# A 64-batch cross attention and mixture kernel: the cross attention's phase turned by half a step

## The reference, cut to what matters

```python
q = (layernorm(x) @ Wq).reshape(B, Nq, 8, 64)
k = (context @ Wk)...; v = (context @ Wv)...
attn = softmax(einsum('bihd,bjhd->bhij', q, k) * 64 ** -0.5)
x = x + einsum('bhij,bjhd->bihd', attn, v).reshape(B, Nq, 512) @ Wo + bo

h = layernorm(x)
rw = gating(h, sim_matrix, gates)          # 16 experts, softmax over the active ones, the best 2 if none is
q, k, v = [einsum('bte,bted->btd', rw, einsum('btc,ecd->bted', h, w)) for w in (q_proj, k_proj, v_proj)]
attn = causal_softmax(q @ k.T / 8) @ v
x = x + einsum('bted,edc->btc', attn[:, :, None, :] * rw[..., None], o_proj)
```

## Time and profile before

| | |
|---|---|
| median of 3 runs | 3160.13 us (3153.86 to 3162.54) |
| the profiled execution | 3160.58 us, its span 3158.8 us |
| TensorE, VectorE, ScalarE, GpSimd busy | 2698.7, 2240.8, 1329.0, 1095.7 us |
| the mean granted TensorE clock | 0.929 of full speed |
| DMA | 440.76 MB, 140 GB/s |

### The profile page before, as it was taken

The page is one execution under the profiler, slowest core; times in us unless marked ns, Lnnn a source line. Parts: engine busy times, 40 slices in busy tenths (PEclk is TensorE's granted clock), DMA queues, the critical chain, the costliest instruction groups (busy, mean ns, idle before and its releaser), DMA issues. The chain is left out here.

```text
span 3158.8 us, 54354 instructions
## 1 busy us (share of the span) xinstructions
PE 2698.7 (85%) x17290; PEld 2574.5 (82%) x17290; DVE 2240.8 (71%) x6487; ACT 1329.0 (42%) x4594; POOL 1095.7 (35%) x1675
## 2 busy tenths in 40 slices
PE   4688889888888889888888889898888888898897
PEld 3688878888888878888888888788888888788886
DVE  5476777676777777777676767676777767676774
ACT  4443444343443444444343444443444434444431
POOL 0142333342333333343333333333433423333443
PEclk6799999999999999999899999898999999999998
DMA  6554444444444454445453444534454544444431
GB/s 155 166 161 127 147 146 133 150 144 143 135 153 129 150 147 129 150 150 153 125 153 119 150 136 137 152 123 144 148 154 126 162 126 147 144 129 147 150 104 38
DMA packets 296557, 440.76 MB, mean 140 GB/s; under 512 B 36752, under 2 KB 208720, under 8 KB 288080
## 3 DMA queue, kind: packets, MB, share of 16 engines
q1 hardware_dynamic: 296272, 437.28, 45.8%
HBM read 257.91 MB, written 179.31 MB: 138 GB/s over the span
## 5 line engine op out<-in xcount | busy, mean ns | idle before, releaser
L1263 DVE SCALAR_TENSOR_TENSOR acc<-bank_b,rw,acc 128x192 f32<-128x192 f32 x1792 | 647.0, 407 | 273.1 <-PE bank_b L506 269.1
L504 PE MATMUL bank_b<-wqkv_hi,x2T_lo 128*128 128x384 f32 (+1 forms) x2048 | 742.6, 363 | 93.2 <-DVE acc L1263 92.2
L506 PE MATMUL bank_b<-wqkv_hi,x2T_hi 128*128 128x384 f32 (+1 forms) x2048 | 718.0, 351 | 0.0
L505 PE MATMUL bank_b<-wqkv_lo,x2T_hi 128*128 128x384 f32 (+1 forms) x2048 | 717.7, 350 | 0.0
L1539 POOL TENSOR_TENSOR mixs_lo<-mix,mixs_hi 128x512 fp32r<-128x512 f32 x256 | 362.1, 1434 | 437.1 <-ACT mixs_hi L996 437.1
L504 PEld LDWEIGHTS bank_b<-wqkv_hi,x2T_lo 128*128 128x128 f32 x2048 | 409.7, 200 | 119.5 <-DVE acc L1263 105.5
L1458 POOL TENSOR_TENSOR pow_out<-pow_in,expo 128x2 f32<-128x2 f32 (+1 forms) x128 | 111.1, 868 | 907.9 <-DVE pow_in L1104 621.0
L505 PEld LDWEIGHTS bank_b<-wqkv_lo,x2T_hi 128*128 128x128 f32 x2048 | 408.4, 199 | 0.0
L506 PEld LDWEIGHTS bank_b<-wqkv_hi,x2T_hi 128*128 128x128 f32 x2048 | 405.6, 198 | 0.0
L940 ACT ACTIVATE probs<-bank_a,s_max 128x77 f32<-128x77 f32 x1024 | 318.2, 333 | 71.0 <-DVE s_max L1191 70.9
L1304 DVE TENSOR_TENSOR mix<-rw_all,late_tiles 128x512 f32<-128x512 f32 x256 | 267.3, 1064 | 80.3 <-DMA rw_all<-rw_dram 78.1
(11 more groups left out here) (201 smaller groups left out, 6371.5 us busy)
## 6 DMA issues: line engine op xcount, KB each, us to landing
gq<-g_dram SPq DMA_DIRECT2D x64, 1232.0 KB, 8.5
g_dram<-draft SPq DMA_DIRECT2D x168, 462.0 KB
uo<-u_dram SPq DMA_DIRECT2D x64, 1024.0 KB
rw_all<-rw_dram SPq DMA_DIRECT2D x128, 512.0 KB, 6.1
u_dram<-draft SPq DMA_DIRECT2D x172, 308.0 KB
xt<-in_x_dram SPq DMA_DIRECT2D x64, 256.0 KB, 5.9
out_dram<-mix SPq DMA_DIRECT2D x64, 256.0 KB, 2.3
uo<-u_dram SPq DMA_DIRECT2D x64, 208.0 KB
```

The source lines that it names most:

```text
L504: nc.tensor.matmul(dst, lhs[1], rhs[0], start=start, stop=False)
L505: nc.tensor.matmul(dst, lhs[0], rhs[1], start=False, stop=False)
L506: return nc.tensor.matmul(dst, lhs[0], rhs[0], start=False, stop=stop)
L1263: V.scalar_tensor_tensor(acc[:, t, k, :], src, rw[:, t, e:e + 1], acc[:, t, k, :], ALU.mult, ALU.add).then_inc(b_evac, 1)
```

## The change: what it does

It moves the cross attention by half a step against the mixture. In step i TensorE now works on XT of batch i+2 (`nxt`), and on S, PT and Y of batch i+1 (`ahead`). The score tiles stand in the first half of the step, one each behind fills 7, 8, 9 and 10, among the quarters of `c_y`; PT0 to PT2 among fills 12 to 14; Y between fill 2 and `c_pv`, where the scores were. LayerNorm 2 of batch i moves to the step's start. The jobs are dealt anew over the places, M3 being filled in one step of three (before: in all three), M2 in all (before: in two).

Other parts: ScalarE now issues the transfers of the routing weights itself, the write right behind the transposition, which moves to the step's first half, and the spread load behind PT1's copy (`c_rw`). LayerNorm 2's result, qkv and p2 now lie in `mix`, the small attention's operands in `mixs`, and `x2` in three tiles in turn, so GpSimd's copy of it (line 1474) goes. `b_route` is cut in two, the causal scores' maximum between them. Group 0 becomes a full group of three batches, and the last group holds batch 63 alone but is computed as three. The diff, cut:

```diff
-    GROUPS = (B - 1) // GB + 1
+    GROUPS = (B + GB - 1) // GB
...
-    A_ORDER = ("E0", "PT0", "PT1", "PT2", "E1", "Y", "E2", "E3", "M1", "XT", "M2", "M3", "S0", "S1", "S2", "S3", "L1", "L2")
+    A_ORDER = ("E0", "S0", "S1", "S2", "S3", "E1", "E2", "PT0", "PT1", "PT2", "E3", "M1", "XT", "M2", "M3", "Y", "L1", "L2")
...
+    JOBS = ({"E0": ("g", 3), "E1": ("k", 3), "E2": ("g", 4), "E3": ("g", 5), "M1": ("v", 0), "M2": ("g", 6), "L1": ("g", 7),
+             "L2": ("v", 1)},
...
+        gm = i // 3 + (2 if kind == "ct" or i % 3 == 2 and kind != "u" else 1)
...
+        qkv = mix[:, 0:2, :].rearrange("p a b -> p (a b)")[:, 0:NT * QKV].rearrange("p (t f) -> p t f", t=NT)
+        x2n = mix[:, 2:2 + NT, :]
+        p2 = mix[:, 4:6, :].rearrange("p a b -> p (a b)")[:, 0:3 * P]
+        k_hi, q_stack, k_stack = [mixs[0][:, k, :] for k in range(3)]
+        v2 = [mixs[0][:, 4 + k, :].rearrange("p (t a d) -> p t a d", t=NT, a=2) for k in range(2)]
+        p2T = [mixs[1][:, 2 * k:2 * k + 2, :].rearrange("p a b -> p (a b)")[:, 0:3 * P].rearrange("p (a b) -> p a b", a=3)
+               for k in range(2)]
...
+            def step(i):
+                def turn(slot):
+                    if job(i, slot):
+                        gm, kind, f = job(i, slot)
+                        if kind == "g":
+                            store_g(gm, f)
+                        elif kind == "u":
+                            store_u(gm, f)
+                if i % 3 == 2 and i // 3 + 3 < GROUPS:
+                    load_ctx(i // 3 + 3)
+                turn("E0")
+                if on(i + 2) and i + 2 > 0:
+                    load_x(i + 2)
+                if on(i + 2):
+                    load_g(i + 2)
+                turn("E1")
+                if i % 3 == 2 and on(i + 1):
+                    load_u(i + 1)
+                if on(i - 2):
+                    store(i - 2)
+                turn("E2")
+                turn("E3")
+                turn("M1")
+                turn("M2")
+                turn("M3")
+                if i % 3 != 1 and on(i + 2):
+                    load_u(i + 2)
+                turn("L1")
+                turn("L2")
...
                 do(before, b_qkv, 6)
-                turn("E0", (j_v, 2), (j_ct,), (j_k, 3))
+                turn("E0")
+                do(before, c_rT)
                 do(before, b_qkv, 7)
                 do(earlier, c_y, 0)
+                fill("S0", ahead, a_s, 0)
                 do(before, b_qkv, 8)
+                fill("S1", ahead, a_s, 1)
                 do(earlier, c_y, 1)
-                fill("PT0", now, a_pT, 0)
-                fill("PT1", now, a_pT, 1)
+                do(before, b_qkv, 9)
+                fill("S2", ahead, a_s, 2)
+                do(before, b_qkv, 10)
+                fill("S3", ahead, a_s, 3)
                 do(earlier, c_y, 2)
-                fill("PT2", now, a_pT, 2)
+                do(before, b_qkv, 11)
+                turn("E1")
                 do(earlier, c_y, 3)
-                do(before, b_qkv, 9)
-                turn("E1", (j_u, 2), (j_k, 0), (j_g, 4))
-                do(before, b_qkv, 10)
-                fill("Y", now, a_y, 0)
-                do(before, b_qkv, 11)
-                turn("E2", (j_u, 3), (j_k, 1), (j_g, 5))
-                do(now, a_y, 1)
+                turn("E2")
                 do(before, b_qkv, 12)
-                turn("E3", (j_v, 3), (j_g, 0), (j_v, 0))
+                fill("PT0", ahead, a_pT, 0)
+                fill("PT1", ahead, a_pT, 1)
                 do(before, b_qkv, 13)
+                fill("PT2", ahead, a_pT, 2)
                 do(before, b_qkv, 14)
+                turn("E3")
                 do(before, b_qkv, 15)
-                turn("M1", (j_u, 4), (j_g, 1), (j_g, 6))
-                fill("XT", ahead, a_xT)
-                do(before, c_rT)
                 do(now, b_xT, 0)
                 do(now, b_xT, 1)
-                turn("M2", (j_u, 5), (None,), (j_g, 7))
+                turn("M1")
+                fill("XT", nxt, a_xT)
+                turn("M2")
                 do(before, c_qk)
                 do(now, b_qkv, 0)
-                turn("M3", (j_u, 6), (j_k, 2), (j_v, 1))
+                turn("M3")
                 do(now, b_qkv, 1)
                 do(before, c_s)
                 do(now, b_qkv, 2)
-                fill("S0", ahead, a_s, 0)
-                fill("S1", ahead, a_s, 1)
-                fill("S2", ahead, a_s, 2)
+                fill("Y", ahead, a_y, 0)
                 do(before, c_pT)
-                fill("S3", ahead, a_s, 3)
+                do(ahead, a_y, 1)
                 do(before, c_pv)
                 do(now, b_qkv, 3)
                 do(now, b_qkv, 4)
-                turn("L1", (j_u, 7), (j_g, 2), (j_u, 0))
+                turn("L1")
                 do(now, b_qkv, 5)
-                turn("L2", (None,), (j_g, 3), (j_u, 1))
-
-            for r in (1, 2):
-                step(-1, r)
-            for i in range(B + 2):
-                step(i // 3, i % 3)
+                turn("L2")
...
             def c_rT(n):
-                act.wait_ge(c_fill, c_at(n, C_RT))
-                if not (known(n) and n == 0):
-                    act.wait_ge(rwT_out, 16 * n)
-                nc.scalar.activation(rwT[:, :], bank_c(C_RT)[0:E, 0:T], copy).then_inc(rwT_ready, 1)
+                act.wait_ge(rT_fill, at(1, n, 0))
+                if n:
+                    act.wait_ge(mix_lo, at(4, n - 1, 0))
+                nc.scalar.activation(rwT[:, :], bank_rT[0:E, 0:T], copy).then_inc(rwT_ready, 1)
+                act.wait_ge(rwT_ready, at(1, n, 0))
+                nc.scalar.dma_start(rw_dram[:, :], rwT[:, :]).then_inc(rwT_out, 16)
+            def c_rw(n):
+                act.wait_ge(rwT_out, 16 * (n + 1))
+                if n:
+                    act.wait_ge(mix_ready, at(4, n - 1, 3))
+                for k in range(2):
+                    nc.scalar.dma_start(rw_all[k * D:(k + 1) * D, :, :],
+                                        rw_dram[:, :].rearrange("(a k) t -> k a t", k=2)[k].partition_broadcast(D)).then_inc(rw_all_in, 16)
...
+                turn("E0")
+                do(before, c_rT)
+                do(ahead, a_exp, 0)
+                do(ahead, a_exp, 1)
+                do(ahead, a_exp, 2)
+                do(ahead, a_exp, 3)
+                turn("E1")
+                turn("E2")
+                do(ahead, a_pT, 0)
+                do(ahead, a_pT, 1)
+                do(before, c_rw)
+                do(ahead, a_pT, 2)
+                turn("E3")
                 do(now, b_xT, 0)
                 do(now, b_xT, 1)
+                turn("M1")
+                do(nxt, a_xT)
+                turn("M2")
                 do(before, c_qk)
+                turn("M3")
                 do(before, c_exp)
                 do(now, b_exp)
                 do(before, c_pT)
                 do(before, c_pv)
                 do(before, c_mix, 0)
                 do(before, c_mix, 1)
                 do(before, c_mix, 2)
+                turn("L1")
                 do(before, c_mix, 3)
+                turn("L2")
...
                 do(before, b_qkv, 6)
+                turn("E0")
                 do(before, b_qkv, 7)
+                do(now, ln2_a)
+                do(ahead, a_s, 0)
                 do(before, b_qkv, 8)
+                do(ahead, a_s, 1)
+                do(now, ln2_b)
+                do(before, b_qkv, 9)
+                do(ahead, a_s, 2)
+                do(now, b_norm, 0)
+                do(before, b_qkv, 10)
+                do(now, b_norm, 1)
+                do(ahead, a_psum, 0)
+                do(ahead, a_s, 3)
+                do(now, b_norm, 2)
+                do(ahead, a_psum, 1)
+                do(before, b_qkv, 11)
+                turn("E1")
                 do(earlier, c_y)
+                turn("E2")
+                do(nxt, ln1_a)
                 do(before, b_qkv, 12)
+                do(ahead, a_pT, 0)
+                do(ahead, a_pT, 1)
                 do(before, b_qkv, 13)
+                do(ahead, a_pT, 2)
+                do(nxt, ln1_b)
                 do(before, b_qkv, 14)
+                turn("E3")
                 do(before, b_qkv, 15)
                 do(now, b_xT, 0)
                 do(now, b_xT, 1)
+                turn("M1")
+                do(nxt, a_xT)
+                turn("M2")
                 do(before, c_qk)
+                do(now, b_top)
                 do(before, c_s)
+                do(now, b_index)
                 do(before, c_p)
+                turn("M3")
+                do(before, c_pT)
                 do(now, b_wsum)
                 do(now, b_qkv, 0)
                 do(now, b_qkv, 1)
+                do(ahead, a_y)
+                do(before, c_mix, 0)
                 do(now, b_qkv, 2)
+                do(before, c_mix, 1)
                 do(now, b_qkv, 3)
+                do(before, c_mix, 2)
                 do(now, b_qkv, 4)
                 do(before, c_mix, 3)
```

(13 more changed lines are left out.)

534 lines of the change are left out of this document (204 added, 330 removed).

## The result

The changed kernel takes 2812.94 us (median of 4 runs, 2811.70 to 2814.86), against 3161.24 us before: a ratio of 0.890, with an interval of 0.889 to 0.892.

What follows compares the result with a forecast made beforehand. TensorE's waits were taken to set the time, VectorE next at 72% of a step. Profiled 3160.6 - 313 (waits removed) + 50 + 31 + 62 - 80 (clock) + 10 (ends) = 2920.6 us; predicted 2920, range 2820 to 3110.

Steps and rivals of the forecast that it cites:

- the clock: TensorE's loss at 1.2 GHz, 166 us: half returns as waits shrink, 80 us off; bounds 0 and 150.
- The exponentials: TensorE's waits for score exponentials before S3, context and K jobs: all 132.7 us go.
- The sums: Mixture fills waiting for VectorE's sums: 80 of 92.2 us go, as the spread load is issued earlier.
- Y's wait for `uo`: Output product Y waiting for its tile by DMA: 40 of 57.3 us off; bounds 57 off, 105 on.
- The sum of q, k, v: TensorE's wait for the sum of q, k and v: nearly the same cover, 15 of 44.7 us off.
- `c_s`: Causal scores wait for `c_qk`'s four ScalarE copies and two subtractions: 50 us added; bounds 0 and 100.
- Fills 3 to 7: VectorE has a `c_mix` part ahead of each fill from 2 to 5: 0.5 us a step, 31 us added.
- The end of the first half: VectorE's added work there makes TensorE wait at fill 15, `b_xT` and `c_qk`: 1.0 us a step, 62 us added.
- rival A: VectorE closes a circle: late maxima delay exponentials, then VectorE and TensorE wait; slower, priced at 3220 us; chance 0.12.
- B: `uo` comes late for Y each third step, behind `gq` and routing weights: 105 us of waits, 3045 us; chance 0.09.
- D: TensorE's wait moves to ScalarE's block of sixteen exponentials and stays, the clock keeps falling: about 3160 us; chance 0.06.
- C: `c_mix` parts block whole on the VectorE-GpSimd port, VectorE sets the second half's pace: 3055 us; chance 0.13.

Runs made afterwards that it cites:

- a_together: Changed kernel with score tiles S0 to S3 directly behind each other after the first quarter of `c_y`; 3073.41 us, ratio 0.974.
- b_early: Kernel before, with only the routing weights' transposition, write and spread load moved to the step's start, still on SyncE's queue; 3046.49 us, ratio 0.966.
- a_late: Changed kernel with the routing weights' spread load issued late, behind the copy of the small attention's transposed probabilities; 3268.14 us, ratio 1.036.
- a_gap: Changed kernel with `c_s` directly behind `c_qk` on TensorE, ahead of two fills and a job that stood between; 3076.72 us, ratio 0.976.
- a_best: a_ln plus job M2's copies put behind `c_qk` on ScalarE and behind `c_p` on VectorE; 2824.86 us, ratio 0.896.
- b_gapfill: Kernel before, with unread products in two waits for exponentials: six ahead of S3, eight ahead of a job in two of three steps; 3112.02 us, ratio 0.988.
- b_swap: Kernel before, with S3's maximum and exponentials put ahead of the first part of `c_mix` on VectorE and ScalarE; 3145.95 us, ratio 0.999.
- a_ln: Changed kernel with VectorE's statistics of the next batch moved earlier, ahead of the second half's reciprocal; 2858.56 us, ratio 0.907.

## Why the prediction was wrong

The chain of causes was right, the waits came out close in sum, and the step that failed is **one term of the sum: the clock, "I give back half of the 166 us: 80"**. The profiled pair gives back 162 us, above even the bound of 150, and the mean of all executions some 143. Term by term, by the profiled pair:

- *The exponentials, 132.7 off:* 129 off. That S3's wait goes by the scores' spacing is shown by a_together (154.3 us return); the 62 us before the jobs already go with the early load alone (b_early).
- *The sums, 80 of 92.2 off, as the load is early:* at the fills nothing is left but the 18.1 us named below, and the reason was wrong. With the early load alone (b_early) the wait stayed at 95.1. It went with the rest of the new order; which part of it was not tested apart, so that the term came out is luck. That the new order needs the early load is shown by a_late: 455 us more with a load issued 3.7 us ahead of its use.
- *Y's wait for `uo`, 40 of 57.3 off:* 39.4 off. Softmax, 45 of 53.6: 49.7 off. The sum of q, k, v, 15 of 44.7: 31.4 off, 16 us better than I took it.
- *`c_s`, +50:* 60.9, and it waits for the two subtractions, as said.
- *Fills 3 to 7, +31:* 18.1, and not for the reason given. These waits are for the first pair's sums (L1232), for which VectorE waits 26.7 us for the routing weights, a delay that I had put at nothing. For the sums behind the parts of `c_mix` (L1235) it is one wait of 0.2 us. *The end of the first half, +62:* 52.6 at `b_xT` and, which I had not priced, 34.7 at the K and U jobs for the lower half of PT; 87 in all.
- Waits together: forecast 170 us off, measured 178.5. That they agree is in part luck: the sum of q, k, v and the fills were better than I took them, the end of the first half and `c_s` worse. *Ends, +10:* the rest beside waits and clock is 5 off.
- *Clock, -80:* -162.

With 162 in place of 80 and the rest of the sum untouched, the forecast would have been 2839 us (2858 with 143), inside the range that it gave. The low end has a fault of its own: half of the added waits and 130 us of clock make 3160.6 - 313 + 71.5 - 130 + 10 = 2799 us, below the time that came, but I closed the range at 2820. The main fault was to let the loss shrink as the sum of the waits does (380 to 210, a little under half). The loss does not follow the sum. 3.04 us of waits a step, 96% of it in pieces under 1.5 us, cost 0.06 us of clock in the changed kernel, and one wait of 3.3 us in place of the 1.0 at `c_s` cost 2.5 (a_gap). a_best waits 3.06 us a step, as much as the changed kernel, but has 31 waits of 1.5 us and more in the 56 steps, not 3, and loses 0.61. Nor does it follow the longest wait alone, as the pair of 0.75 and 1.14 us shows. I had a row for the long ones: the 0.54 us behind the 2.30 us gap, and in rival A I even priced one such gap at 1.7 us. I did not look for what stood ahead of the other falls. 132.7 us of waits of up to 3.7 us were to go, and b_gapfill shows 1.85 of 2.86 us a step behind these and the pair.

The rivals. **A** (VectorE's circle) did not happen: VectorE waits 87.3 us for the exponentials, 1.4 a step, and TensorE waits for them about 3 us in the whole run. **B** did not: Y waits 17.9 us, not 105. **D** did not, though b_swap shows that waits can move and their sum stay. **C** (the parts of `c_mix` wait for a whole GpSimd instruction each, and VectorE sets the pace) did not. VectorE's timeline of the changed kernel has the four parts, here from the second on:

```profile
1436.91 0.68 DVE L1276 TENSOR_TENSOR mix<-rw_all,late_tiles 128x512 f32<-128x512 f32 x1
...
1438.16 1.13 DVE L1276 TENSOR_TENSOR mix<-rw_all,late_tiles 128x512 f32<-128x512 f32 x1
...
1439.87 1.13 DVE L1276 TENSOR_TENSOR mix<-rw_all,late_tiles 128x512 f32<-128x512 f32 x1
```

and GpSimd's remainders, taken one by one, begin in between:

```profile
1437.09 1.66 POOL L1511 TENSOR_TENSOR mixs_lo<-mix,mixs_hi 128x512 fp32r<-128x512 f32 x1 [3.43 <-ACT mixs_hi L961]
1438.71 1.75 POOL L1511 TENSOR_TENSOR mixs_lo<-mix,mixs_hi 128x512 fp32r<-128x512 f32 x1
1440.40 1.75 POOL L1511 TENSOR_TENSOR mixs_lo<-mix,mixs_hi 128x512 fp32r<-128x512 f32 x1
1442.12 1.29 POOL L1511 TENSOR_TENSOR mixs_lo<-mix,mixs_hi 128x512 fp32r<-128x512 f32 x1
```

Three parts lie beside GpSimd, as I had counted. But the second was running when GpSimd began and keeps its 0.68 us. The third and fourth begin with 0.59 us of a GpSimd instruction left to run, and each costs 0.45 us more than alone, not the 0.7 that I took nor the 1.43 of rival C. GpSimd pays too: its instruction takes 1.29 us with no part beside it and 1.66 to 1.75 with one. My 1.40 was the mean of two unlike parts. One by one, the last of them in the kernel before and the GpSimd instruction that it meets are

```profile
1463.45 1.77 DVE L1304 TENSOR_TENSOR mix<-rw_all,late_tiles 128x512 f32<-128x512 f32 x1
```

```profile
1463.35 1.32 POOL L1539 TENSOR_TENSOR mixs_lo<-mix,mixs_hi 128x512 fp32r<-128x512 f32 x1 [0.37 <-ACT mixs_hi L996]
```

so with 1.22 us of it left the part costs 1.09 more. In both kernels together 254 parts begin beside a running GpSimd instruction, and each of them ends 0.54 to 0.56 us behind that instruction's end.

The Trainium skill ("SBUF — State Buffer", section "SBUF: two separate sides") says that of a VectorE and a GpSimd instruction that need the shared ports the one that starts first has them for its whole length, and the other is blocked. I had read this as a full instruction lost each time, 134 us in all, and the trace disagrees with that. Read as the rest of the instruction already running, the trace agrees: 0.59 us left and 0.45 us more, 1.22 left and 1.09 more.

## What to carry to other kernels

Price a wait of the matrix engine twice: its length, and what the engine then runs at 1.2 GHz; and take the second from what stands ahead of each fall of the clock, by the matmuls behind it, not from the sum of all waits. In the 56 steps of all fourteen traces here the clock fell 460 times: 375 times behind a wait of 1.7 us or more, 85 times behind two shorter ones with less than 1.5 us of work between them. Not every such wait or pair had a fall behind it. Such a wait must be split or covered, and such a pair pulled apart, before short waits that lie further apart. Before a step is moved into another engine's idle time, look up on the DMA queue when its input is issued: the gain meant in a_ln was turned into a loss by a load that had been early enough for the old order, and most of it came back when the queue was turned as well (`uo`'s longer wait stayed).

## What the hardware showed that I had not expected

- Useless matmuls make a kernel with a long wait faster: 640 of them, 104 us (0.943 [0.941, 0.944] against 0.976 [0.974, 0.977]); in the kernel before, 728 gained 43 us. Neither comes near the changed kernel (0.890), in which the wait is not there.
- The clock's price was not of one size: 1.56 us a step behind waits of 2.45 us (a_together), 2.47 behind waits of 3.3 us (a_gap), 0.06 in the changed kernel, where a step's 3.04 us of waits are mostly pieces under 1.5 us. And a pair of 0.75 and 1.14 us, 0.5 us apart, had the clock fall behind it in 32 of 55 steps.
- A VectorE instruction that meets a running GpSimd one here waits for the rest of it and no more: it ended 0.54 to 0.56 us behind the other's end 254 times of 254. GpSimd's own goes from 1.29 to 1.66 or 1.75 us.
